# A two-layer perceiver on one core: projections moved between the start, the stage between the layers and the first block of layer 1

## The reference

```python
def _layernorm(x, axis=-1, eps=1e-05):
    m = jnp.mean(x, axis=axis, keepdims=True)
    v = jnp.var(x, axis=axis, keepdims=True)
    return (x - m) / jnp.sqrt(v + eps)
...
        q = _split_heads(hidden_states_query @ Wq.T + bq)      # 16 heads of 16
        k = _split_heads(hidden_states_key @ Wk.T + bk)
        v = _split_heads(hidden_states_key @ Wv.T + bv)
        scores = jnp.einsum('bhqd,bhkd->bhqk', q * scale, k)
        scores = scores + ((1.0 - attention_mask) * -10000.0)[:, None, :, :]   # layer 0 alone
        probs = jax.nn.softmax(scores, axis=-1)
        ctx = jnp.einsum('bhqk,bhkd->bhqd', probs, v)
...
    x = x + _L0_xattn_ref(_layernorm(x, axis=-1), ctx_1024, mask_BxSxS2_ff1, ...)   # cross-attention
    x = x + _L0_attn_ref(_layernorm(x, axis=-1), ...)    # causal linear attention, then a GELU MLP
    x = x + _L0_ffn_ref(_layernorm(x, axis=-1), ...)     # gated MLP, quantized inputs and weights
    x = x + _L1_xattn_ref(_layernorm(x, axis=-1), ctx_1024, ctx_1024, ...)   # the same, no mask, with Wo
    x = x + _L1_attn_ref(_layernorm(x, axis=-1), ...)    # RWKV mixing (a scan)
    x = x + _L1_ffn_ref(_layernorm(x, axis=-1), ...)     # quantized MLP with a convolution
    return x
```

## Time and profile before

| | us |
|---|---|
| median of 3 runs | 965.04 (963.46 to 966.1) |
| profiled execution, own time | 969.17 |
| its span | 966.3 |
| PE busy in the span | 924.5 (96%) |
| DVE, ACT, POOL busy | 755.6, 697.8, 398.6 |
| last weighing of layer 0 begins | 460.10 |
| scores of block 13's tile 0 begin | 521.34 |

### The profile page before, as it was taken

The page is one execution under the profiler, slowest core; times in us unless marked ns, Lnnn a source line. Parts: engine busy times, 40 slices in busy tenths (PEclk is TensorE's granted clock), DMA queues, the critical chain, the costliest instruction groups (busy, mean ns, idle before and its releaser), DMA issues.

```text
span 966.3 us, 37466 instructions
## 1 busy us (share of the span) xinstructions
PE 924.5 (96%) x16290; PEld 572.3 (59%) x16291; DVE 755.6 (78%) x1610; ACT 697.8 (72%) x1005; POOL 398.6 (41%) x365
## 2 busy tenths in 40 slices
PE   7999999999999999999888899999999999999987
PEld 3455665665656566655563556666666666666666
DVE  5888888888888888967446988777777778777666
ACT  3678998998998899897563456666666666666752
POOL 4368888788888877886100010021202000110000
PEclk9999999999999999999997999999999999999999
DMA  8411201201211110123005001011101101000000
GB/s 337 165 42 67 88 26 68 90 24 68 89 60 55 67 58 8 68 91 134 6 26 193 2 2 46 3 45 46 45 4 46 46 3 46 14 3 3 3 1 6
DMA packets 14995, 53.08 MB, mean 55 GB/s; under 512 B 4336, under 2 KB 5744, under 8 KB 10992
## 3 DMA queue, kind: packets, MB, share of 16 engines
q1 hardware_dynamic: 14832, 50.70, 15.1%
HBM read 50.56 MB, written 0.13 MB: 52 GB/s over the span
## 4 chain that ended last, share of the span: by engine, by line
PE 83%; DVE 7%; issue 5%; ACT 3%; DMA 1%; POOL 0%; SPq 0%; DVEq 0%; POOLq 0%; ACTq 0%
PE ps_out L1599 18%; PE ps_scores L1578 16%; PE ps_proj L1501 15%; PE ps_proj L1516 14%; PE ps_max L1523 7%; PE ps_scores L1574 4%; DVE tile_max L1102 2%; ACT probs L821 1%; PE ps_proj L1523 1%; DVE probs L1194 1%; PE ps_scores L1516 1%; DMA bq<-in_L_xattn_bq 1%; DVE unread L1099 1%; PE ps_out L1477 1%; PE ps_max L1477 1%
## 5 line engine op out<-in xcount | busy, mean ns | idle before, releaser
L637 POOL TENSOR_TENSOR probs<-probs,masks 128x512 f32<-128x512 f32 x180 | 227.3, 1284 | 76.3 <-ACT probs L807 76.3
L815 ACT ACTIVATE probs<-probs 128x1024 f32<-128x1024 f32 x196 | 206.7, 1055 | 44.7 <-DVE probs L1183 34.1
L1578 PE MATMUL ps_scores<-q_pad,k_full 32*128 32x256 f32 x3072 | 237.3, 378 | 0.0
L1099 DVE CUSTOM_DVE_ANT_0 unread<-ps_max,masks 128x512 bf16<-128x512 f32 (+1 forms) x294 | 190.5, 675 | 49.1 <-PE ps_max L1523 48.2
L821 ACT ACTIVATE probs<-ps_scores 128x1024 f32<-128x1024 f32 x192 | 186.3, 1021 | 44.8 <-PE ps_scores L1578 44.4
L1599 PE MATMUL ps_out<-probs,values 128*32 128x128 f32 x6272 | 217.1, 277 | 1.6 <-DVE ps_out L1166 0.5
L1578 PEld LDWEIGHTS ps_scores<-q_pad,k_full 32*128 32x128 f32 x3072 | 187.0, 187 | 12.5
L1599 PEld LDWEIGHTS ps_out<-probs,values 128*32 128x32 f32 x6272 | 159.3, 110 | 57.3 <-issue 50.4
L1501 PE MATMUL ps_proj<-wv,ctx_t 128*32 128x256 f32 x2752 | 165.3, 381 | 0.2
L1523 PE MATMUL ps_max<-k_high,q_high 32*128 32x512 bf16 (+1 forms) x579 | 153.2, 382 | 8.5 <-DVE tile_max L1099 3.2
L1516 PE MATMUL ps_proj<-ctx_t,wk 128*32 128x512 f32 (+1 forms) x1360 | 159.8, 587 | 1.0 <-DVE tile_max L1099 0.8
(11 more groups left out here) (308 smaller groups left out, 940.8 us busy)
## 6 DMA issues: line engine op xcount, KB each, us to landing
ctx_t<-in_ctx_t SPq DMA_DIRECT2D x23, 1024.0 KB, 5.9
masks<-in_mask_n SPq DMA_DIRECT2D x12, 512.0 KB, 3.7
masks<-in_mask_t SPq DMA_DIRECT2D x12, 512.0 KB, 3.9
room_w<-in_L_attn_f_w SPq DMA_DIRECT2D x2, 1024.0 KB, 7.0
room_w<-in_L_ffn_w SPq DMA_DIRECT2D x2, 1024.0 KB, 8.1
ctx_t<-in_ctx_t SPq DMA_DIRECT2D x2, 512.0 KB, 5.7
room_w<-in_L_ffn_w_gate SPq DMA_DIRECT2D x1, 1024.0 KB, 11.1
room_w<-in_L_ffn_w_up SPq DMA_DIRECT2D x1, 1024.0 KB, 13.6
```

Of the source, the lines that this page charges most:

```text
L637: nc.gpsimd.tensor_tensor(p, p, three(mask_t[m % 2], GT)[:, t, :].unsqueeze(1).to_broadcast([P, 4, P]), ALU.add).then_inc(sig("bias_added" ...
L815: nc.scalar.activation(prob(T, half), prob(T, half), ACT.Exp).then_inc(sig(f"exp_done{half}"), 1)
L1099: ins = v.tensor_tensor_reduce(unread[:, j % 2, 0:width(m)], max_bank(m, j)[:, 0:width(m)], mask_n[m % 2][:, half_cols(m, half)], 1.0, -3e ...
L1578: last = mm(banks[g][:, D * c:D * (c + 1)], k_full[m % 3][rows, c, P * t:P * (t + 1)], q_pad[rows, c, :], start=False, stop=True, skip_gro ...
```

## The change

The query bias is loaded ahead of the key weights. In `FIRST_AT` key unit 1 goes behind the first four products (it stood ahead of them), units 4 and 5 stand together, and unit 11 goes from ahead of the maxima's turn into tile 0 of block 0, on PE and on ACT. Between the layers nine units are projected instead of thirteen, beside block 13's products four instead of three, and three value units of block 14 in block 13's tiles 3, 5 and 7 (`values_at`). Some copies on ACT move behind steps of the chain. DVE waits for the product last. At the turn of block 13's maxima there are four unread products ahead of it instead of one, and two behind.

```diff
@@ -314,3 +314,3 @@
             k = m + 1
-            if t in VALUES_AT and k < BLOCKS and k not in (NG, NG + 1) and VALUES_AT[t] < value_units(k):
+            if t in VALUES_AT and k < BLOCKS and k != NG and (k, t) != (NG + 1, 1) and VALUES_AT[t] < value_units(k):
                 return k, VALUES_AT[t]
@@ -430,11 +430,11 @@
 
-        FIRST_AT = ((2,), (3,), (4,), (5,), (6, 7), (8,), (9,), (10, 11))
+        FIRST_AT = ((1,), (2,), (3,), (4, 5), (6, 7), (8,), (9,), (10,))
 
 
-        BETWEEN = [("k", NG + 1, 0), ("k", NG + 1, 1), ("v", NG, 0), ("v", NG, 1), ("v", NG, 2), ("k", NG + 1, 2), ("k", NG + 1, 3),
-                   ("k", NG + 2, 0), ("v", NG, 3), ("v", NG + 1, 0), ("v", NG + 1, 1), ("v", NG + 1, 2), ("k", NG + 2, 1)]
+        BETWEEN = [("k", NG + 1, 0), ("k", NG + 1, 1), ("v", NG, 0), ("k", NG + 1, 2), ("k", NG + 1, 3), ("v", NG, 1),
+                   ("k", NG + 2, 0), ("k", NG + 2, 1), ("v", NG, 2)]
 
 
-        BESIDE = [("k", NG + 2, 2), ("k", NG + 2, 3), ("v", NG + 1, 3)]
-        BESIDE_AT = (2, 5, 7)
+        BESIDE = [("v", NG, 3), ("k", NG + 2, 2), ("k", NG + 2, 3), ("v", NG + 1, 0)]
+        BESIDE_AT = (1, 3, 5, 7)
 
@@ -522,5 +522,5 @@
             load_q_weights(0)
+            row(bq[0][:, :], "L0_xattn_bq", D, "q_bias0")
             load_k_weights(0)
             load_first_ctx(0)
-            row(bq[0][:, :], "L0_xattn_bq", D, "q_bias0")
             load_first_ctx(1)
@@ -856,3 +856,3 @@
                 if l == 1:
-                    between_out(12)
+                    between_out(8)
                 turned(4 * l, ps_max[:, 0, 0:D], xn_t[:, :, :].rearrange("p c t -> p (c t)"))
@@ -885,4 +885,2 @@
                     nc.scalar.activation(stat[:, 41:42], ones[:, 0:1], ACT.Exp).then_inc(sig("exp_loaded"), 1)
-                if l == 0:
-                    first_out(len(FIRST) - 1)
                 for n in range(NG):
@@ -904,2 +902,4 @@
                                 mask_bias(m + 1, t - 4)
+                            if T == 0:
+                                first_out(len(FIRST) - 1)
                             exp_in_place(m, t, 0)
@@ -926,3 +926,2 @@
                     turned_scaled(1, ln1_w, ln1_b)
-                    between_out(2)
                     act.wait_ge(sig("feat_min"), 1)
@@ -931,9 +930,7 @@
                     nc.scalar.copy(feat_t[0:FEAT, :], ps_max[0:FEAT, 0, 0:D]).then_inc(sig("feat_t_ready"), 1)
-                    between_out(3)
+                    between_out(2)
                     turned(2, ps_max[:, 0, 0:D], xn_t[:, :, :].rearrange("p c t -> p (c t)"))
-                    between_out(4)
                     ln_root(3)
-                    between_out(5)
                     turned_scaled(3, ln2_w, ln2_b)
-                    between_out(6)
+                    between_out(3)
                     for c in range(FC):
@@ -947,5 +944,6 @@
                     nc.scalar.activation(stat[:, 30:31], ones[:, 0:1], ACT.Silu).then_inc(sig("table_loaded"), 1)
-                    between_out(7, 8)
+                    between_out(4)
                     act.wait_ge(sig("xq_turned"), 1)
                     nc.scalar.copy(bigt.bitcast(BF16)[:, 0:D], ps_max[:, 0, :].bitcast(BF16)[:, 0:D]).then_inc(sig("xq_ready"), 1)
+                    between_out(5)
                     for half in range(2):
@@ -955,3 +953,3 @@
                                              scale=stat[:, 20:21]).then_inc(sig("silu_ready"), 1)
-                    between_out(9, 10, 11)
+                    between_out(6, 7)
                     for half in range(2):
@@ -1093,7 +1091,8 @@
                     need("max_chain", stage(m))
-                dve.wait_ge(sig("max_ready"), J + 1)
-                if m < NG:
-                    if j == 0:
+                    if m < NG:
                         dve.wait_ge(sig(f"mask_n_loaded{m % 2}"), m // 2 * 16 + 16)
+                if m < NG:
                     need("max_free", J - 1)
+                dve.wait_ge(sig("max_ready"), J + 1)
+                if m < NG:
                     ins = v.tensor_tensor_reduce(unread[:, j % 2, 0:width(m)], max_bank(m, j)[:, 0:width(m)], mask_n[m % 2][:, half_cols(m, half)],
@@ -1698,4 +1697,4 @@
                 if l == 1:
-                    between_read(11)
-                    between_read(12)
+                    between_read(7)
+                    between_read(8)
                 for zz in range(2):
@@ -1711,3 +1710,2 @@
 
-                    first_in(1)
                 pe.wait_ge(sig("q_copied"), 2 * l + 1)
@@ -1724,9 +1722,14 @@
                             beside_in(BESIDE_AT.index(i))
-                    beside_read(1)
+                    for u in (len(BESIDE) - 2, len(BESIDE) - 1):
+                        if u % 2 == 1:
+                            beside_read(u)
                 read_by[0] = ("max_copied", NG * l + 1)
                 if l == 1:
-                    idle_products(1, ps_proj)
+                    idle_products(4, ps_proj)
                 turn_max(NG * l, ps_proj)
                 if l == 1:
-                    beside_read(2)
+                    for u in (len(BESIDE) - 2, len(BESIDE) - 1):
+                        if u % 2 == 0:
+                            beside_read(u)
+                    idle_products(2)
                 if l == 0:
@@ -1746,2 +1749,4 @@
                             weigh(m - 1, size(m - 1) - 1)
+                        elif l == 0:
+                            first_in(len(FIRST) - 1)
                         turns(m, t)
@@ -1769,3 +1774,3 @@
                 if l == 0:
-                    between_in(0, 1, 2)
+                    between_in(0, 1)
                 pe.wait_ge(sig("sums_taken"), l + 1)
@@ -1779,3 +1784,3 @@
                     project(ps_proj[:, 0:QKV], w_qkv).then_inc(sig("qkv_ready"), 1)
-                    between_in(3)
+                    between_in(2)
                     pe.wait_ge(sig("feat_ready"), 1)
@@ -1789,3 +1794,2 @@
                     mm(ps_proj[:, 0:D + 1], att, vone[:, 0:D + 1], start=True, stop=True).then_inc(sig("num_ready"), 1)
-                    between_in(4)
                     pe.wait_ge(sig("lin_ready"), 1)
@@ -1795,3 +1799,3 @@
                     project(ps_proj[:, 0:D], w_o).then_inc(sig("o_ready"), 1)
-                    between_in(5, 6)
+                    between_in(3)
                     pe.wait_ge(sig("ln2_applied"), 1)
@@ -1809,3 +1813,3 @@
                     last.then_inc(sig("f2_ready"), 1)
-                    between_in(7, 8)
+                    between_in(4, 5)
                     pe.wait_ge(sig("xq_made"), 1)
@@ -1824,3 +1828,3 @@
                             last.then_inc(sig("gate_ready"), 1)
-                    between_in(9, 10, 11)
+                    between_in(6, 7)
                     idle_products(1, ps_proj)
@@ -1837,3 +1841,3 @@
                     last.then_inc(sig("down_ready"), 1)
-                    between_in(12)
+                    between_in(8)
 
```

More of the change, by code:

```diff
@@ L931, in _ @@
                     nc.scalar.copy(feat_t[0:FEAT, :], ps_max[0:FEAT, 0, 0:D]).then_inc(sig("feat_t_ready"), 1)
+                    between_out(2)
+                    turned(2, ps_max[:, 0, 0:D], xn_t[:, :, :].rearrange("p c t -> p (c t)"))
+                    ln_root(3)
+                    turned_scaled(3, ln2_w, ln2_b)
                     between_out(3)
[L933 to L938 removed]
                     for c in range(FC):
```

7 lines of the change are left out of this document (2 added, 5 removed).

## The result

The changed kernel takes 975.81 us (median of 4 runs, 975.69 to 979.07), the kernel before 965.57 in the same comparison (963.46 to 967.57): ratio 1.0115, 95% interval 1.0097 to 1.0134. It is slower by 10 us; I had forecast 962.0.

The account below looks back on a forecast made before the run. PE was taken as the bound in layer 0's steady loop, DVE in block 13. Terms 1.5 - 4.7 + 1.5 - 3.9 + 2.6 = -3.0 gave a median of 962.0 us, range 958.0 to 966.5.

Parts of the forecast that it names:

- DVE's waits in another order: DVE's waits ahead of its maxima: the new order costs 0, within 0.5 us either way.
- Start: Start and block 0: first maximum earlier, but POOL's late mask addition delays tile 2; +1.5 us, bounds -1.2 and +3.0.
- Between the layers: Stage between layers 0 and 1: nine projections instead of thirteen let PE's turns come earlier; -4.7 us.
- rival (d): Between the layers: PE's clock falls, +8 us at most, 968 to 970 us; chance 0.10.
- Turn of layer 1's maxima: Layer 1's first maxima: fourth unit's copy and four unread products delay the turn; +1.5 us, bounds +0.4 and +2.
- Clock in tiles 0 and 1: Block 13, tiles 0 and 1: added PE work keeps the clock full; -3.9 us, bounds 0 and -5.7.
- rival (a): Block 13: plain runs mostly lack the low clock, so its term is near 0; 965.9 us, chance 0.21.
- Three value units in block 13: Block 13, tiles 3, 5, 7: each added value projection is partly hidden, costing 0.9; +2.6 us, bounds 0 and 5.2.
- rival (c): Block 13: the added projections aren't hidden at all, +5.2 us, 964.6 us; chance 0.10.

Follow-up runs that it names:

- a1: The changed kernel with only the order of DVE's waits ahead of a maximum put back (product, mask, bank of results): 968.82 us, ratio 1.0052.
- b1: The kernel before with only the new order of DVE's waits (mask, bank of results, product): 973.62 us, ratio 1.0094.
- c1: The kernel before with only the change's new start (bias load first, key units 1, 4, 5 and 11 moved): 968.42 us, ratio 1.0040.
- c3: The changed kernel with the order of waits put back and the unread products at layer 1's turn as before: 967.89 us, ratio 1.0027.
- b2: The kernel before with only the mask's wait moved ahead of the product's wait, at a block's first maximum: 964.76 us, ratio 1.0001.
- b3: The kernel before with a long-met wait for the query bias written first ahead of layer 0's maxima, except each block's first: 972.54 us, ratio 1.0084.
- s2: The kernel before with the new start alone, POOL's first mask addition put ahead of its cast of unit 11's keys: 965.92 us, ratio 1.0018.
- s3: The kernel before with the new start alone, unit 11 put back ahead of the turn of the maxima: 965.46 us, ratio 1.0015.
- c2: The kernel before with only the move of the projections (nine units between the layers, three value units in block 13): 964.14 us, ratio 1.0000.
- w2: The kernel before with the move of the projections, and the last-met wait first at blocks' first maxima and mask additions in tiles 0, 4: 963.98 us, ratio 0.9990.

## Why the prediction was wrong, point by point

**DVE's waits in another order: 0, within 0.5. This step failed**, and it decides the sign. I priced whether a wait is met, not which instruction carries it. The order of the instructions showed the swap; I called it free because "all waits were met in program order anyway". In the steady loop PE was called the bound with DVE idle, and I took DVE's start times for free; but PE's last product of each tile hangs on DVE's first maximum. Measured: 7.0 in the changed kernel (less a1), +9.0 alone (b1, up to 1.6 of it clock); 6.3 in blocks 1 to 11 of the profile.

**Start, +1.5.** The mechanism was right; the size was low, and c1's 4.1 lies above the upper bound of 3.0. Changed kernel, PE, DVE and POOL, for the earlier trace rows:
```profile
5.96 2.05 PE L1462 MATMUL ps_proj<-wq,xn_t 128*128 128x256 f32 x4
7.94 2.34 PE L1515 MATMUL ps_scores<-ctx_t,wk 128*32 128x512 f32 x16
...
38.28 0.40 PE L1573 MATMUL ps_scores<-max_rows,minus 32*128 32x512 bf16 x4 [0.42 <-issue]
...
47.08 0.64 PE L1598 MATMUL ps_out<-probs,values 128*32 128x128 f32 x16 [1.58 <-ACT probs L815]
...
49.85 0.60 PE L1573 MATMUL ps_scores<-max_rows,minus 32*128 32x512 bf16 x4
```
```profile
8.14 0.42 DVE L1215 TENSOR_TENSOR room_t<-ps_proj,bq 128x256 f32<-128x256 f32 x1 [2.82 <-PE ps_proj L1462]
...
12.42 0.69 DVE L1098 CUSTOM_DVE_ANT_0 unread<-ps_scores,masks 128x512 bf16<-128x512 f32 x1 [3.36 <-PE ps_scores L1522]
```
```profile
42.42 1.04 POOL L628 CAST k_high<-k_full 128x1024 bf16<-128x1024 f32 x1 [7.07 <-ACT k_full L750]
43.43 2.51 POOL L637 TENSOR_TENSOR probs<-probs,masks 128x512 f32<-128x512 f32 x2
```
The bias is added at 8.14, the first maximum is at 12.42 (12.5 forecast), scores of tile 0 at 38.28 (as before, as forecast), the mask addition at 43.43 (43.3), tile 2 at 49.85 (49.4; the wait is the 1.58 at 47.08). Two things I missed. The query projection took 2.05 and not 1.13. The trace's record of full clock begins at 8.8 there, and at 5.9 in the profile of the earlier trace rows; in 15 of the 18 profiles of this study it begins between 7.8 and 11.7, so the reference was an odd one. And the new start costs 4.1 in plain runs (c1), but only 1.5 and 2.1 at block 1's first exp in the profiles of a1 and c3 (against b2). c1's profile is 4.0 late there: it has a stretch of 3.4 us at half clock from 54.9, which costs 1.6. None of its six runs has a mean clock above 0.998, where 44 of 96 runs of the kernel before have 0.999. But the profiles of b1 and b3 have the same stretch with the old start, and those of the changed kernel, a1, c3, s2 and s3 lack it with the new one. So what brings it stays open, and part of c1's 4.1 with it.

**Between the layers, -4.7.** Changed kernel, for the earlier trace rows:
```profile
475.84 0.30 PE L1457 MATMUL ps_scores<-ident,xn 128*128 128x128 f32 x1 [0.18 <-DVE xn L1301]
...
483.06 0.52 PE L1451 MATMUL ps_max<-ident,room_t 128*128 128x128 f32 x2 [0.59 <-DVE room_t L1319]
484.04 2.08 PE L1462 MATMUL ps_proj<-room_w,xn_t 128*128 128x256 f32 x4 [0.46 <-ACT xn_t L727]
485.91 2.27 PE L1486 MATMUL ps_out<-ctx_t,wk 128*128 128x512 f32 x4
488.44 0.33 PE L1457 MATMUL ps_scores<-ident,xn 128*128 128x128 f32 x1 [0.26 <-DVE xn L1029]
```
The turns come right behind DVE, as forecast: the first 1.4 earlier against the last weighing, the second 1.0 more. Then the output projection takes 2.08 and not 1.13, the key unit 2.27. The clock is 0.50 from 483.3 to 486.7. Ahead of it, from 480.0 to 483.1, PE had only the short turn and products of the attention, with 0.44 to 0.59 idle between them; in the kernel before a value unit stood there (474.32 to 476.2 of its trace), and the clock stayed full. This is rival (d), at a smaller size. All five profiles of kernels with nine units (after, a1, c2, c3, w2) have such a stretch that begins 14 to 16 us behind layer 0's last exp, none of the thirteen others has. Its cleanest picture is c3:
```profile
477.03 1.36 PE L1461 MATMUL ps_proj<-room_w,xn_t 128*128 128x256 f32 x4 [0.46 <-ACT xn_t L727]
478.19 3.38 PE L1485 MATMUL ps_out<-ctx_t,wk 128*128 128x512 f32 x4
481.41 0.27 PE L1456 MATMUL ps_scores<-ident,xn 128*128 128x128 f32 x1
```
1.36 for 1.13, 3.38 for 1.88: some 1.7 us. From layer 0's last exp to layer 1's first it is 62.9 in kernels with thirteen units and full clock, 59.7 in c3: -3.2, and -4.9 without the stretch. The sizes of the projections were right; the clock gave a third of them back, and three fifths where the stretch was 6.8 us long (c2, w2: -1.9 in all).

**Turn of layer 1's maxima, +1.5.** Changed kernel, for the earlier trace rows:
```profile
525.78 1.99 PE L1676 MATMUL ps_proj<-wq,ident 128*128 128x256 f32 x8 [0.70 <-ACT values L758]
527.71 0.41 PE L1617 MATMUL ps_proj<-ident,max_of_head 128*32 128x128 bf16 x16
528.04 1.13 PE L1676 MATMUL ps_out<-wq,ident 128*128 128x256 f32 x4
529.11 0.39 PE L1573 MATMUL ps_scores<-max_rows,minus 32*128 32x512 bf16 x4
```
Last reduction 526.00, turn 527.71: 1.71 where it was 0.49; and 1.40 from there to tile 0 where it was 1.14. +1.5, as forecast; a1 against c3 gives 1.5 in the profiles too, and too little in the medians to tell.

**Clock in tiles 0 and 1, -3.9.** Changed kernel, tiles 0, 1, 3 and 5, for the earlier trace rows:
```profile
529.11:532.72 3.61, 2.76 (x29) 1.47 (x29) 2.04 (x4) 3.08 (x4) 0.00 (x0) 1.00 0.01 2
532.72:536.42 3.70, 3.30 (x61) 2.16 (x59) 3.69 (x7) 1.94 (x2) 0.00 (x0) 1.00 0.00 0
541.73:548.82 7.09, 6.60 (x108) 4.29 (x108) 4.31 (x7) 2.42 (x3) 1.16 (x1) 0.79 0.01 2
553.07:557.83 4.76, 4.69 (x91) 2.91 (x91) 4.22 (x8) 2.16 (x3) 0.00 (x0) 1.00 0.01 3
```
3.61 and 3.70 at clock 1.00: 7.3 for 7.4 forecast. But that was no gain, because the profile that I counted against isn't typical. The profile of b2, tiles 0, 1, 3, 5 and 7:
```profile
522.03:525.66 3.63, 2.77 (x29) 1.55 (x30) 2.05 (x4) 3.24 (x4) 0.00 (x0) 1.00 0.33 140
525.66:529.35 3.69, 3.29 (x60) 2.15 (x59) 3.68 (x7) 1.94 (x2) 0.00 (x0) 1.00 0.00 0
534.66:538.64 3.98, 3.40 (x75) 2.52 (x75) 3.74 (x7) 2.42 (x3) 0.18 (x1) 1.00 0.00 0
542.96:546.63 3.67, 3.27 (x59) 2.01 (x59) 3.58 (x7) 1.94 (x2) 0.00 (x0) 1.00 0.00 0
550.55:554.64 4.09, 3.51 (x75) 2.45 (x75) 3.85 (x7) 2.42 (x3) 0.30 (x1) 1.00 0.00 0
```
Full clock without the unread products. Of the thirteen profiles with thirteen units, six have a low stretch that begins with tile 0 (within 0.3 us of its scores); four of these are 6.8 us long, the other two 10.2. Of 96 plain runs of the kernel before, eight had a mean clock as low as the profiled one's 0.992. That was rival (a), to which I gave 0.21: with "the profiled one lies 4.1 above their median" in hand it was the likelier reading.

**Three value units in block 13, +2.6.** Tiles 3, 5 and 7 of c3, whose block 13 has full clock:
```profile
533.19:539.22 6.03, 5.21 (x107) 3.32 (x108) 4.22 (x7) 2.42 (x3) 1.15 (x1) 1.00 0.01 3
543.47:548.23 4.76, 4.69 (x90) 2.91 (x90) 4.22 (x8) 2.16 (x3) 0.00 (x0) 1.00 0.02 3
552.07:558.09 6.02, 5.20 (x107) 3.31 (x107) 4.42 (x8) 2.64 (x4) 2.14 (x2) 1.00 0.01 3
```
+2.05, +1.09 and +1.93 against b2: 4.6 for the block by its exps. Tile 5 is near my 0.9. Tiles 3 and 7 hold a turn of maxima, and there nothing is hidden. I had taken the slack of tile 5 for all three; rival (c) in size. Block 14 gives 0.4 back. In the changed kernel tile 3 takes 7.09 us at clock 0.79 where c3's takes 6.03, so its block 13 is another 1.1 longer, 5.7 in all. Four of the five profiles with nine units have this stretch in tile 3, and four of the thirteen others one there too; the prediction had left it as it was.

So the parts other than the waits come to +4 (a1) or about +5 (their sum), not -3: the start 4.1 (for 1.5), the units 0 (for -2.1: -4.7 and +2.6), the unread products 0.6 in the medians and 1.5 in the profile (for -2.4: +1.5 and -3.9).

## What to carry to other kernels

Where an instruction waits for several things, write the wait that is met last first, and read from the trace which wait the instruction carries; here it was the one written first. "Busy 100%" doesn't say that an engine is free of waits: compare the length of one round and follow the reuse of its banks. Before a term rests on a stretch of low clock in one profile, look whether the plain runs have it; here their mean clock said no.

## What the hardware showed that I had not expected

A DVE maximum whose product is awaited by a semaphore instruction of its own starts 0.53 us behind PE's product, one that carries the wait itself 0.42; over blocks 1 to 11 that made 6.3 us. Two bf16 products on different rows of PE take 0.39 us as neighbours, 0.31 each when apart. Taking four projections out of the stage between the layers brought a stretch at half clock there in five profiles of five, though PE stood idle for no longer than 0.6 us at a time in the 3 us ahead of it (changed kernel, 480.0 to 483.3).
